# Order of TensorE's broadcasts and of VectorE's small steps in the closing phase of a two-layer kernel

## The reference

```
x = L0_attn_x
xn = _layernorm(x, axis=-1)
s = _L0_attn_ref(xn, ...)      # two-level wavelet split, linear attention, synthesis, layernorm
g = _silu(_L0_ffn_ref(xn, ...))  # ternary weights: silu(a)*b, two gelu layers of 1024, projection to 256
x = x + s * g
xn = _layernorm(x, axis=-1)
s = _L1_attn_ref(xn, ...)
g = _silu(_L1_ffn_ref(xn, ...))
x = x + s * g
```

```
dA = jnp.exp(d_t[:, :, None] * A)
dBx = d_t[:, :, None] * b_t[:, None, :] * x_t[:, :, None]
h = dA * h + dBx
y = jnp.einsum('bhn,bn->bh', h, c_t)
```

```
logits = einsum(normed, gate_weight) + gate_bias ; scores, idx = top_k(logits, 2) ; w = softmax(scores)
p1 = einsum(normed, mlp1_weight) + mlp1_bias
g = jnp.minimum(p1[..., 0::2], LIMIT)
lin = jnp.clip(p1[..., 1::2], -LIMIT, LIMIT)
act = g * jax.nn.sigmoid(ALPHA * g) * (lin + 1.0)
p2 = einsum(act, mlp2_weight) + mlp2_bias ; combined = sum of p2 * combine over the experts
```

## Time and profile before

| what | value |
|---|---|
| median of 3 runs | 1988.3 us (1987.76 to 1990.13) |
| the profiled execution, its own time | 1990.13 us |
| its span, first to last instruction | 1988.4 us |
| PE busy, share of the span | 1502.8 us, 76% |
| DVE busy | 1507.2 us, 76% |
| ACT busy | 1133.0 us, 57% |
| POOL busy | 905.7 us, 46% |
| mean granted clock of TensorE | 0.888 |

### The profile page before, as it was taken

How to read it: one execution, slowest core, us unless ns; L and a number is a source line. 1 busy time by engine, 2 the same in 40 slices (tenths; PEclk the granted TensorE clock), 3 DMA queues, 4 the chain that set the end, 5 groups by cost and what they waited for, 6 DMA issues and landing times.

```text
span 1988.4 us, 16440 instructions
## 1 busy us (share of the span) xinstructions
PE 1502.8 (76%) x5296; PEld 638.0 (32%) x5296; DVE 1507.2 (76%) x1822; ACT 1133.0 (57%) x1515; POOL 905.7 (46%) x578
## 2 busy tenths in 40 slices
PE   5898887689887768888888758868888664563777
PEld 1443433334432323333333223333443221111322
DVE  2673288788588958979768868878948897998964
ACT  3546667675535568667525556866553544445545
POOL 3141344445018763554206764454502874474454
PEclk8999999899988879999988879999998886686879
DMA  7000000001000000000100010000100200000000
GB/s 179 1 32 22 11 1 0 22 0 60 15 0 32 22 22 0 22 1 1 64 11 21 12 42 1 0 22 1 64 11 0 95 22 21 0 0 0 0 11 11
DMA packets 12599, 42.42 MB, mean 21 GB/s; under 512 B 1866, under 2 KB 1890, under 8 KB 10466
## 3 DMA queue, kind: packets, MB, share of 16 engines
q1 hardware_dynamic: 11698, 35.08, 4.8%
q0 software_dynamic: 816, 6.30, 1.4%
HBM read 38.23 MB, written 4.19 MB: 21 GB/s over the span
## 4 chain that ended last, share of the span: by engine, by line
PE 40%; DVE 26%; ACT 16%; issue 12%; POOL 5%; DMA 0%; POOLq 0%; SPq 0%; DVEq 0%; ACTq 0%
PE psf L1392 8%; PE psf L1383 6%; ACT da L1007 3%; DVE st L2123 3%; PE psu L1566 3%; PE psy L1551 3%; PE psf L1305 2%; PE psu L1667 2%; PE psf L1362 2%; PE psy L1362 2%; DVE lin L2254 2%; POOL ap L752 2%; ACT L1007 2%; ACT L895 2%; PE psu L1305 2%
## 5 line engine op out<-in xcount | busy, mean ns | idle before, releaser
L729 POOL TENSOR_TENSOR gx<-gx,sy 128x1024 f32<-128x1024 f32 x120 | 304.3, 2536 | 236.4 <-DVE sy L2137 236.4
L747 POOL TENSOR_TENSOR gate<-gate,lin 128x512 f32<-128x512 f32 x120 | 161.9, 1349 | 404.2 <-DVE lin L2261 399.1
L1085 ACT ACTIVATE gate<-gate 128x512 f32<-128x512 f32 x128 | 80.5, 629 | 225.7 <-DVE gate L2250 225.5
L2108 DVE TENSOR_TENSOR psu<-so,psu 128x1024 f32<-128x1024 f32 x128 | 156.6, 1224 | 44.5 <-PE psu L1505 44.1
L720 POOL TENSOR_TENSOR g2p<-tf,g2p 128x512 fp32r<-128x512 f32 x64 | 85.9, 1346 | 221.6 <-ACT g2p L926 221.5
L1392 PE MATMUL psf<-g1p,h2w 128*128 128x512 f16 x768 | 177.7, 379 | 4.9 <-ACT tf L903 4.9
L1392 PE MATMUL psf<-hp,h1w 128*128 128x512 f16 x768 | 176.0, 379 | 5.8 <-ACT tf L895 5.8
L1007 ACT ACTIVATE da<-delta,aneg 128x512 f32<-128x512 f32 x256 | 163.6, 710 | 28.3 <-DVE so L2103 21.9
L1667 PE MATMUL psu<-ap,mw 128*128 128x512 f16 x384 | 117.3, 436 | 72.7 <-POOL ap L752 72.4
L2123 DVE TENSOR_TENSOR_SCAN st<-da,carry,psu 128x512 f32<-128x512 f32 x128 | 156.8, 1267 | 6.8 <-ACT carry L1013 5.0
L2137 DVE TENSOR_TENSOR sy<-st,psu 128x1024 f32<-128x1024 f32 x128 | 156.0, 1219 | 6.8 <-DVE st L2123 2.6
(11 more groups left out here) (368 smaller groups left out, 3337.5 us busy)
## 6 DMA issues: line engine op xcount, KB each, us to landing
mw<-in_mlp_w SPq DMA_DIRECT2D x3, 2048.0 KB, 8.2
xn<-in_x SPq DMA_DIRECT2D x8, 512.0 KB, 6.4
wf<-in_wf SPq DMA_DIRECT2D x4, 1024.0 KB, 4.7
xr<-in_x SPq DMA_DIRECT2D x8, 512.0 KB, 3.9
x<-gx SPq DMA_DIRECT2D x8, 512.0 KB, 3.8
out<-outc SPq DMA_DIRECT2D x8, 512.0 KB, 3.1
mw<-in_mlp_w SPq DMA_DIRECT2D x3, 1024.0 KB, 10.3
h1w<-in_h POOLq DMA_DIRECT2D x1, 2048.0 KB, 12.8
```

What stands on the lines that cost most here:

```text
L729: pool.tensor_tensor(out, chunk(gx, c), sy[:, n % 2], ALU.add).then_inc(y_acc.sem, 1)
L747: pool.tensor_tensor(gate[:, r % NG], gate[:, r % NG], lin_at(b, r)[:], ALU.mult)\
L2108: dve.tensor_tensor(input_banks(n), chunk(so, c), both(psu[:, row_bank(n)]), ALU.mult)\
```

## The change

Only the four `closing` functions are edited; every instruction that ran still runs, with the same operands, in another order on its engine.

- POOL: `gated_out(b, 0)` and `expert_out(b, 0)` both stand ahead of the expert tiles of chunk 1; before, `expert_out` stood after five of them.
- ACT and PE, second loop: `hidden1` and `hidden2` of chunk 0 run one state later.
- PE, first loop, n = 8 to 15: `spread_c` stands ahead of the early tile's `expert_up`, and `expert_spread` for the next step stands at the end of a step, behind the late tile's `expert_up`; before, it stood in the next step behind the early tile's `expert_up`.
- PE, last loop: `expert_spread` for the next two tiles stands directly behind the `expert_up` of every odd i; before, it stood ahead of the `expert_up` of every even i, behind the downs and the feed-forward matmuls of the tile between. `expert_down` stands ahead of `hidden1`. The first broadcast of chunk 1 is issued in the second loop at n = 8.
- DVE: `head_z0` of chunk 1 moves from inside `expert_weights` to behind the scan of state 6, `head_z1` from there to behind the input of state 7, `expert_parts` to behind the scan of state 7. `block_out(b, 0)` moves from state 14 of the second loop to behind it.

```
@@ POOL closing
+                gated_out(b, 0, b)
+                expert_out(b, 0)
                 for r in range(NQ, Q):
-                    if r == NQ:
-                        gated_out(b, 0, b)
-                    if r == NQ + 5:
-                        expert_out(b, 0)
                     expert_product(b, r)
@@ ACT closing
-                    if 5 <= n < 5 + KF:
-                        hidden1(b, 0, n - 5)
+                    if 6 <= n < 6 + KF:
+                        hidden1(b, 0, n - 6)
@@ PE closing
                 for n in range(NS):
+                    spread_c(b, 0, n)
                     pair = expert_pair(n)
                     if pair:
                         expert_up(b, pair[0], b)
-                        expert_spread(b, n - 8, b)
-                    spread_c(b, 0, n)
-                    if pair:
                         for r in (pair[0] - 3, pair[0] - 2):
...
                     if pair:
                         expert_up(b, pair[1], b)
+                        if n + 1 < NS:
+                            expert_spread(b, n - 7, b)
...
+                    if n == 7:
+                        expert_spread(b, 0, b)
...
-                    if 5 <= n < 5 + KF:
-                        hidden1(b, 0, n - 5, False)
+                    if n == 8:
+                        expert_spread(b, E, b)
                     if 6 <= n < 6 + KF:
-                        hidden2(b, 0, n - 6)
+                        hidden1(b, 0, n - 6, False)
+                    if 7 <= n < 7 + KF:
+                        hidden2(b, 0, n - 7)
                 for i in range(NQ + 3):
                     if i < NQ:
-                        if i % KD == 0:
-                            expert_spread(b, E + i // KD, b)
                         expert_up(b, NQ + i, b)
                     if i == 0:
                         lf_average(b, 1, False)
+                    if i % KD == KD - 1 and 1 <= i // KD + 1 < E:
+                        expert_spread(b, E + i // KD + 1, b)
                     if i == 2:
                         lf_variance(b, 1)
+                    if i >= 3:
+                        expert_down(b, NQ + i - 3)
                     if 5 <= i < 5 + KF:
                         hidden1(b, 1, i - 5, False)
-                    if i >= 3:
-                        expert_down(b, NQ + i - 3)
                     if 6 <= i < 6 + KF:
                         hidden2(b, 1, i - 6)
@@ DVE closing (the two functions beside_* become one that takes a list)
-                        if at == CHOICE_STEPS + 3 and c == 0:
-                            head_z0(b, 1)
...
                 state_scan(b, 0, 6)
-                head_z1(b, 1)
+                head_z0(b, 1)
                 state_output(b, 0, 6)
                 state_input(b, 0, 7)
+                head_z1(b, 1)
+                state_scan(b, 0, 7)
                 expert_parts(b, 0)
-                state_scan(b, 0, 7)
                 state_output(b, 0, 7)
...
                 for n in range(7, NS):
                     state_step(1, n)
                     if n == 7:
                         expert_parts(b, 1)
-                    if n == NS - 2:
-                        block_out(b, 0)
+                block_out(b, 0)
```

More of the change, by code:

```diff
@@ L2380, in state_step, with beside_gate @@
                     state_output(b, c, n)
-                def beside_choice(c):
+                def beside_gate(c, steps):
                     def beside(at):
[L2385 to L2397, removed]
-                        if at == CHOICE_STEPS + 3 and c == 0:
-                            head_z0(b, 1)
[L2400 to L2403, removed]
+                        for when, piece, n in steps:
+                            if at == when:
+                                piece(b, c, n)
                     return beside
@@ L2411, in closing @@
                 state_input(b, 0, 3)
-                expert_choice(b, 0, beside_choice(0))
+                expert_choice(b, 0, beside_gate(0, ((2, state_scan, 3), (6, state_output, 3), (10, state_input, 4))))
                 state_scan(b, 0, 4)
@@ L2417, in closing @@
                 state_input(b, 0, 5)
-                expert_weights(b, 0, beside_weights(0))
+                expert_weights(b, 0, beside_gate(0, ((14, state_scan, 5), (18, state_output, 5), (22, state_input, 6))))
                 state_scan(b, 0, 6)
-                head_z1(b, 1)
+                head_z0(b, 1)
                 state_output(b, 0, 6)
                 state_input(b, 0, 7)
+                head_z1(b, 1)
+                state_scan(b, 0, 7)
                 expert_parts(b, 0)
-                state_scan(b, 0, 7)
                 state_output(b, 0, 7)
@@ L2444, in closing @@
                 state_input(b, 1, 3)
-                expert_choice(b, 1, beside_choice(1))
+                expert_choice(b, 1, beside_gate(1, ((2, state_scan, 3), (6, state_output, 3), (10, state_input, 4))))
                 state_scan(b, 1, 4)
@@ L2449, in closing @@
                 state_input(b, 1, 5)
-                expert_weights(b, 1, beside_weights(1))
+                expert_weights(b, 1, beside_gate(1, ((14, state_scan, 5), (18, state_output, 5), (22, state_input, 6))))
                 state_scan(b, 1, 6)
```

## The result

The changed kernel takes 2020.5 us (median of 4 runs, 2017.28 to 2024.67) where the kernel before, on the same chip, takes 1988.7. The ratio is 1.0161, with a 95% interval of 1.0140 to 1.0181: 32 us slower (28 to 36). The forecast was 2015.5 us, which is 27.2 us slower, with a range of 2004 to 2026.

What follows compares the result with a forecast made beforehand. DVE was taken to bound the expert half of the first loop and the second loop, PE the last. Terms 4.7 + 0.6 + 5.9 + 10.0 + 0.3 + 2.4 + 3.3 = 27.2 us on 1988.3 gave 2015.5, range 2004 to 2026.

Steps and rivals of the forecast that it cites:

- the start of the last loop: Last loop, PE at i = 3 and 5: a replaced wait costs 0.3 us, a later up(6') costs 2.4.
- the clock: Last loop, PE: half of four new stalls followed by a stretch at 1.2 GHz, 3.3 us (0 to 7).
- head_z0 and head_z1: First loop, DVE: stalls of 4.7 us ahead of state_output(6) and 0.6 from the late z1.
- The first loop's order: First loop, n = 7 to 15: DVE waits for expert_up ahead of the early gate clip, 5.9 us in all.
- four bare steps: First loop, steps to n = 12 to 15: uncovered DVE stalls, each 0.6 us at higher clock, 1.9 at lower.
- The steps with cover, 8 and 10: First loop: other work partly hides DVE's wait, leaving 0.4 to 1.4 us to n = 8, 0 to 0.6 to 10.
- Second loop and POOL: Second loop and POOL's moved expert_out: no cost, zero for each.
- The four stalls of the last loop: Last loop, i = 7, 9, 11, 13: PE waits for DVE's scale ahead of the broadcast, 4 x 2.5 = 10.0 us.
- The rival "the clock holds": Last loop: the new stalls cost PE no clock, total 2010 us (2005 to 2010.5); chance 0.20.
- The rival of the other sign: Not slower: PE's last-loop waits cost nothing, only block_out's move counts, 1.3 us earlier, 1987.0 us; chance 0.04.

Runs made afterwards that it cites:

- e4_rest: Kernel before with hidden1 and hidden2 one state later, block_out behind the last state, chunk 0's POOL output steps ahead of the tiles; ratio 0.9998.
- e3_last: Kernel before with only PE's last loop changed: weight broadcast behind each odd tile's up, down ahead of hidden1, first broadcast in the second loop; 1.0085.
- e8_mid: Kernel before with the changed kernel's PE last loop, but an odd tile's weight broadcast behind its down instead of ahead of it; ratio 1.0042.
- e6_down: Kernel before with only the down put ahead of hidden1 in the last loop; ratio 1.0001.
- a2_again: The changed kernel, unedited, run once more for a second profile; 2033.1 us, one run.
- e7_up: Kernel before with up(1') ahead of lf_average on PE and, on DVE, tile 1' ahead of block_out and lf_center; ratio 0.9992.

## Why the prediction was right

**In short.** The waits were right: DVE's in the first loop, PE's in the last, at the instructions that were named. One term was too small (the start of the last loop, 2.7 against 4.0), and one came out right for a wrong reason (the clock).

**head_z0 and head_z1.** Forecast 4.7 and 0.6, measured 4.79 and 0.93. The chain z0, head_delta1 at half speed, expert_turn, C broadcast is the one that the rows of PE show, with the durations of the earlier trace rows.

**The first loop's order.** Forecast 5.9 from idles of 0.6 and 1.9 at the two levels of the clock; measured 0.50 and 1.76, and 6.5 us in the six steps named. (The sum behind the 0.6 is 0.14 + 0.22 + 0.22 + 1.03 = 1.61, not 1.64; it changes nothing.) The total is partly luck. Three of the four bare steps were at the lower level, where the stage's clock gives fewer than two, so they cost 5.8 us against a forecast of 4.8. The steps with cover, 8 and 10, cost 0.7 against 1.1.

**Second loop and POOL.** Forecast nothing; measured -1.1 us in the profile of e4_rest, not told from nothing by the times. If that is more than chance, the 1.3 us by which lf_average comes earlier are not all lost again, as I had put it.

**The four stalls of the last loop.** Forecast 10.0; two tiles take 2.59 us longer, 10.4 in all. Of each 2.59, 2.44 are idle time; the other 0.15 were not looked into. e3_last, e8_mid and e6_down together show that the place of the broadcast alone does it.

**The start of the last loop.** Forecast 0.3 + 2.4; measured 4.0 in the changed kernel (35.0 against 31.1 us in e4_rest, from state_output(15) to clip 6') and 5.8 in e3_last. This is the term that was mis-sized. I had the place and the wait right: the clips and the scale of 5' delay PE by 2.25 us, as forecast. I had not seen that lf_scale's own two instructions would take 1.65 us longer. PE then needs 5.1 us from the broadcast to up(6'), 0.5 more than it needed from hidden1 before, as it was at the lower clock for nearly all of it. Against that, lf_scale starts 0.5 us earlier in the changed kernel, not 0.3 later; in e3_last it starts 1.2 later, which is most of the difference between 4.0 and 5.8.

**The clock.** Forecast 3.3 as half of four stalls; measured 14.83 + 14.82 - 2 x 13.13 = 3.4. The size is right, the reasoning is not, so the agreement is luck: there is no half chance at each stall. In all three profiles of the changed kernel the same two of the four stalls lose the clock, and in both of e3_last, with the same stalls of 2.44 us, none does. The rival "the clock holds" is thus true of these stalls in e3_last and false in the changed kernel. What decides it is open; a filling in the changed kernel itself was not tried. The prediction also did not ask what the clock does at the last downs, where e3_last and e6_down lose 1.4 us and the changed kernel nothing.

The prediction weighed a rule of the Trainium skill, page "TensorE: Matmul & The Clock Gate", section "Why this matters for your kernels". The idle gaps of 2.44 us are shorter than those it warns of, and behind some of them the clock was at 1.2 GHz, behind others not.

**The sum.** Forecast 27.2; the closing phase of the profiled execution is 29.7 us longer. By terms that is 5.7 and 6.5 in the first loop with 0.7 not assigned, -1.1, 10.4, 4.0 and 3.4. The medians differ by 31.8 (28 to 36), so the 27.2 lies just below the interval. The other 2.1 may lie in the stage ahead of the closing phase, where the same code varies by more than that, or in executions like a2_again; no profile shows which.

**The rival of the other sign** needed slack on PE in the last loop or matmuls that pass a waiting one. e3_last shows PE idle for 2.44 us with ready downs and hidden1 behind the broadcast: nothing passes.

## What to carry to other kernels

In an instruction stream that runs in order, the place of a wait decides what it costs. Put an instruction that waits for another engine's answer as late as its own readers allow, behind all work that is ready, and count the work between question and answer: each microsecond of it comes off the stall. Moving such a wait is free only on an engine that is not the bound in that stage, and which engine is the bound must be read stage by stage. When a wait has been removed, follow the chain to the next engine before timing it, as e7_up shows. And when the parts of a change add up to the whole, compare them stretch by stretch before calling them independent: here the sums agreed and the makeup did not.

## What was not expected of the hardware

**A DVE instruction of 0.54 us took 1.37 beside POOL.** lf_scale's two scale-and-shift instructions (L2154 before, L2156 after: one tensor and two constants per partition) in the kernel before, DVE's timeline:

```profile
1920.52 1.00 DVE L2154 TENSOR_SCALAR nrm<-nrm,pk 128x512 f32<-128x512 f32 x2
```

and in the changed kernel, with POOL's timeline under it:

```profile
1935.57 2.66 DVE L2156 TENSOR_SCALAR nrm<-nrm,pk 128x512 f32<-128x512 f32 x2
```

```profile
1935.06 1.59 POOL L747 TENSOR_TENSOR gate<-gate,lin 128x512 f32<-128x512 f32 x1 [3.11 <-ACT gate L1083]
1936.61 1.33 POOL L752 TENSOR_TENSOR ap_z<-gate,ap_z 128x512 f16<-128x512 f32 x1
```

Before, POOL began its product only inside the second of the pair, and the pair took 1.00 us; here POOL was at work already when each of them began, and they took 2.66 (1.37 each, where it was 0.54), e3_last the same. POOL's product is longer as well, 1.59 where 1.26 is usual. In the kernel before, POOL's timeline:

```profile
1921.24 1.41 POOL L747 TENSOR_TENSOR gate<-gate,lin 128x512 f32<-128x512 f32 x1 [3.12 <-ACT gate L1085]
```

The kernel before also has the slow case, in the second loop, where the same two instructions of chunk 0 begin beside POOL's state_add. DVE's timeline, then POOL's:

```profile
1835.28 2.90 DVE L2154 TENSOR_SCALAR nrm<-nrm,pk 128x512 f32<-128x512 f32 x2
```

```profile
1834.19 3.25 POOL L729 TENSOR_TENSOR gx<-gx,sy 128x1024 f32<-128x1024 f32 x1 [6.07 <-DVE sy L2137]
```

The first of the two took 2.44 us there and the second, which began when POOL was done, 0.54. In the 14 profiles of this case the instruction stands 224 times. In 68 it began while an instruction of POOL ran, and took 1.37 to 2.47 us; in the 156 others it took 0.53 to 0.55, also in the 8 inside which POOL began. The Trainium skill, page "GPSIMD Engine Reference", section "1. Specifications", says that the two engines share their SBUF interfaces and get into each other's way when DVE runs an instruction that uses both of its ports. These rows agree, and they add that the one that began second was lengthened most. No run took POOL's work away from there, but e8_mid comes near to it: with PE's order alone changed, the pair began ahead of POOL's product and took 1.00 us.

**The code ahead of the closing phase** took 1644.3 to 1655.5 us in three profiles of one program. What varies there was not looked for.
